# First attention of a hybrid block: the side work of TensorE in pieces behind even chunks, v in another bank, routing spread over three batches, and the bias table loaded in the tail

## What is computed

```python
scores = g_scale * jnp.einsum('bhqd,bhkd->bhqk', l2norm(q), l2norm(k))         # attn_a
pos = jnp.cumsum(ohf, axis=0) - 1.0; keep = posk < C                           # routing
scores = jnp.einsum('bqhd,bkhd->bhqk', q, k) * scale + position_bias           # attn_b
```

## Time and profile before

| | us |
|---|---|
| median of 3 runs | 1488.24 |
| lowest and highest run | 1486.22, 1497.35 |
| the profiled execution: its own time | 1500.14 |
| its span, first to last instruction | 1498.4 |
| PE busy | 1257.2 (84%) |
| DVE busy | 933.7 (62%) |
| ACT busy | 871.3 (58%) |
| POOL busy | 511.1 (34%) |

### The profile page before, as it was taken

The page is one execution under the profiler, slowest core; times in us unless marked ns, Lnnn a source line. Parts: engine busy times, 40 slices in busy tenths (PEclk is TensorE's granted clock), DMA queues, the critical chain, the costliest instruction groups (busy, mean ns, idle before and its releaser), DMA issues.

```text
span 1498.4 us, 22434 instructions
## 1 busy us (share of the span) xinstructions
PE 1257.2 (84%) x6711; PEld 634.5 (42%) x6711; DVE 933.7 (62%) x2823; ACT 871.3 (58%) x1716; POOL 511.1 (34%) x788
## 2 busy tenths in 40 slices
PE   3888888888749399999999999998999999997292
PEld 2333323332237144454554544544544544544172
DVE  5344555554311278779788698798788788784210
ACT  1777777777514176766656566676566567562041
POOL 2001222222426323323432443343443434424244
PEclk7898999998859699999999999999999999999597
DMA  5554432226349246656656666576575665568322
GB/s 159 113 171 162 131 123 82 89 95 199 97 98 169 51 106 154 161 137 155 166 122 144 166 150 149 132 166 149 136 166 122 149 156 144 117 145 222 83 24 23
DMA packets 132936, 197.91 MB, mean 132 GB/s; under 512 B 35166, under 2 KB 76077, under 8 KB 132816
## 3 DMA queue, kind: packets, MB, share of 16 engines
q1 hardware_dynamic: 104848, 138.67, 35.8%
q0 software_dynamic: 27392, 56.76, 17.9%
q10 hardware_dynamic: 576, 1.05, 0.2%
HBM read 61.75 MB, written 39.24 MB: 67 GB/s over the span
## 4 chain that ended last, share of the span: by engine, by line
PE 64%; DVE 11%; issue 7%; DMA 6%; ACT 6%; POOL 3%; SPq 1%; DVEq 0%; POOLq 0%; ACTq 0%
PE s_ps L1387 13%; PE o_psb L1407 7%; PE o_ps L879 6%; PE o_psb L1412 6%; ACT probs_a L619 5%; PE score_ps L865 4%; PE m_ps L1361 4%; PE m_ps L1378 4%; PE r_ps L1421 3%; PE r_ps L1378 3%; DVE tile L1610 3%; PE p_ps L1395 3%; DVE blocks L1623 2%; DMA x_mid<-o_g_f,rows_f 2%; PE t_ps L894 1%
## 5 line engine op out<-in xcount | busy, mean ns | idle before, releaser
L1523 ACT ACTIVATE tile<-tile,low 128x512 f32<-128x512 f32 x512 | 363.8, 714 | 263.9 <-DVE low L1610 255.0
L1304 POOL DMA_DIRECT2D crossed<-blocks x512 | 253.7, 506 | 505.2 <-DVE blocks L1623 463.5
L1610 DVE CUSTOM_DVE_ANT_0 tile<-s_ps,bias 128x512 f32<-128x512 f32 x512 | 330.5, 682 | 48.7 <-PE s_ps L1387 38.1
L619 ACT ACTIVATE probs_a<-score_ps,gbound 128x1024 f32<-128x1024 f32 x256 | 268.7, 1113 | 105.8 <-PE score_ps L865 105.4
L1387 PE MATMUL s_ps<-kT,qT 64*128 64x512 f32 x1024 | 269.4, 634 | 24.3 <-DVE low L1610 16.6
L1623 DVE STREAM_TRANSPOSE blocks<-tile 128x512 f32<-128x512 f32 x384 | 256.6, 694 | 0.0
L1407 PE MATMUL o_psb<-crossed,v_b 128*64 128x512 f32 x512 | 236.6, 605 | 9.1 <-DMA crossed<-blocks 7.9
L338 POOL DMA_INDIRECT slots<-rows_r,slot_r x128 | 127.8, 998 | 86.7 <-issue 55.0
L879 PE MATMUL o_ps<-probs_a,v_ext 128*32 128x512 f32 x1024 | 153.2, 674 | 0.5 <-ACT probs_a L619 0.5
L1387 PEld LDWEIGHTS s_ps<-kT,qT 64*128 64x128 f32 x1024 | 86.3, 188 | 141.0 <-issue 87.0
L865 PE MATMUL score_ps<-q_stack,k_stack 32*128 32x512 f32 x512 | 100.3, 545 | 39.6 <-ACT probs_a L619 23.4
(11 more groups left out here) (160 smaller groups left out, 1622.4 us busy)
## 6 DMA issues: line engine op xcount, KB each, us to landing
crossed<-blocks SPq DMA_DIRECT2D x512, 96.0 KB
crossed<-blocks POOLq DMA_DIRECT2D x512, 96.0 KB
inv_row<-inv_rows SPq DMA_DIRECT2D x128, 128.0 KB
q_parts<-parts SPq DMA_DIRECT2D x32, 256.0 KB, 3.9
k_stack<-k_parts SPq DMA_DIRECT2D x32, 256.0 KB, 4.4
q_stack<-q_parts SPq DMA_DIRECT2D x32, 256.0 KB, 4.8
w_f<-in_w SPq DMA_DIRECT2D x32, 256.0 KB, 6.4
k_parts<-parts SPq DMA_DIRECT2D x28, 256.0 KB, 4.0
```

What stands on the lines that cost most here:

```text
L619: nc.scalar.activation(probs[q % 2][:, c % 4 // 2, pair:pair + 2, :].rearrange("p h t -> p (h t)"), score_ps[c % 2][:, :], ACT.Exp, bias=g ...
L1304: pool.dma_start(strip_to(n, a, m), strip_from(n, a, m)).then_inc(crossed_sw[n % 2], 16)
L1523: nc.scalar.activation(tile[(b * NS + k) % RING][s][:, :], tile[(b * NS + k) % RING][s][:, :], ACT.Exp, bias=low[n % 2][:, s, i:i + 1], sc ...
L1610: nc.vector.tensor_tensor_reduce(out=tile[(b * NS + k) % RING][s][:, :], in0=s_ps[k % 2][s][:, :], in1=bias[:, h, off:off + S], scale=1.0, ...
```

## The change

- **PE's order in the first attention.** The constants move all side work behind even chunks, between the scores of the two chunks of a pair: x turned behind chunk 0, q and k in two halves behind 2 and 4, v behind 6, q and k turned behind 16; `to_tokens` behind 10 (group 3 of the batch before), 18, 22 and 30; the router's counts behind 22, turn behind 26, logits behind 28. Each `to_tokens` now stands some chunks after the copy that it needs.
- **Banks.** v is made in `t_ps` instead of the upper half of `aux_ps`; so q and k no longer wait for v's copy, and group 3's `to_tokens` waits for it instead. `take` gains a wait for the turn of the group before.
- **Routing over three batches.** Turn, logits and exps stay one batch behind (b - 1); picks, counts and addresses are done two batches behind (b - 2), in the middle of DVE's list. A second signal, `late`, carries those steps. The scatter of batch b - 2 stands behind groups 2 and 3 (three pieces each), its last two pieces in the next batch. In the last batch all that is left is done in a denser order.
- **DVE's list** is rewritten accordingly; the normed rows of batch b + 2 are made at the end of batch b; the Newton steps are split around `take(b, 0)`. SQUARE_AT goes from 9 to 5.
- **Bias table.** Its place in the memory is that of the first attention's q and k buffers. SP loads 6 of its 8 parts when the last scores are done, ahead of the store of the last batch's x, and the last 2 behind the experts' rows.
- **Second attention.** DVE picks the first expert at the end of step 26 and the second at the end of step 28 (both were at 27); ACT's router exp stands at the start of step 26 instead of its end.

```diff
@@ -120,8 +120,8 @@
 
     STATS, MOMENTS, VAR, ROWS, TURNED = TB, 2 * TB, 2 * TB + 1, 3 * TB + 1, 3 * TB + 2
     TOP, SHIFTED = TURNED + 1, TURNED + 2
-    FIRST, SECOND = SHIFTED + 1, SHIFTED + 7
-    CHOSEN = SHIFTED + 12
+    FIRST, SECOND = 1, 7
...
@@ -152,7 +152,8 @@
         self.m, self.addr = own("m", [P, TOPK, TB]), own("addr", [P, TOPK, TB])
         self.slot = [own(f"slot{n}", [P, TOPK, TB], I32) for n in range(bufs)]
         self.const, self.w_in = sem(f"r_const{f}"), sem(f"r_w_in{f}")
-        self.step = Signal(sem(f"r_step{f}"), self.SLOTS)
+        self.step = Signal(sem(f"r_step{f}"), self.SHIFTED)
+        self.late = Signal(sem(f"r_late{f}"), self.SLOTS)
...
@@ -416,9 +421,11 @@
         stacks_in = [Signal(sem(f"stacks_in{i}"), 16 * 2) for i in range(GROUPS)]
         NCH = 32
 
-        AT_PE, SQUARE_AT = [3, 5, 7, 17], 9
-        ROUTE_MORE = dict(turn=23, logits=25, exps=28, counts=31)
-        ROUTE_LAST = dict(turn=13, logits=15, exps=18, counts=25)
+        SQUARE_AT = 5
+        TURN_X, QK_FIRST, QK_SECOND, MAKE_V, TURN_QK = 0, 2, 4, 6, 16
+        TOKENS_MORE, TOKENS_LAST = {10: -1, 18: 0, 22: 1, 30: 2}, {6: -1, 14: 0, 22: 1, 30: 2}
+        ROUTE_MORE = dict(counts=22, turn=26, logits=28, exps=30)
+        ROUTE_LAST = dict(counts=8, turn=18, logits=20, exps=22, own_counts=28)
...
@@ -547,20 +554,21 @@
                 nc.gpsimd.tensor_tensor(rstd[:, lo:hi], var[:, lo:hi], g["neg_half"][:, 0:hi - lo],
                                         ALU.pow).then_inc(ln_rstd, 1)
 
-            def batch(b, before):
-                if before:
-                    r.inverse_std(pool, b - 1)
+            def batch(b):
                 wait(pool, v_staged, b + 1, 1)
                 for grp in range(GROUPS):
                     wait(pool, av_done, b, 2 * grp + 2)
                     pool.sem_inc(g["passed_pool"], 1)
                     move_v(grp)
-                    if b >= 2:
-                        r.scatter(pool, b - 2, range(2 * grp, 2 * grp + 2))
-                    if before and grp == 0:
+                    if grp == 0 and b >= 3:
+                        r.scatter(pool, b - 3, range(6, 8))
+                    if grp == 1 and b >= 3:
+                        r.landed(pool, b - 3)
+                    if grp == 1 and b >= 1:
+                        r.inverse_std(pool, b - 1)
                         r.copy_rows(pool, b - 1)
-                if b >= 2:
-                    r.landed(pool, b - 2)
+                    if grp >= 2 and b >= 2:
...
@@ -718,6 +735,10 @@
 
             def take(b, grp):
                 wait(dve, av_done, b, 2 * grp + 2)
+                if grp >= 1:
+                    wait(dve, oT_ps, b, grp)
+                elif b >= 1:
+                    wait(dve, oT_ps, b - 1, GROUPS)
...
@@ -736,42 +757,57 @@
             turned, logits = aux_ps[:, 0:S], aux_ps[:, S:S + TB * E_N].rearrange("p (t e) -> p t e", e=E_N)
             counts = aux_ps[:, S + TB * E_N:S + 2 * TB * E_N].rearrange("p (t e) -> p t e", e=E_N)
 
-            def batch(b, before):
-                prepare(b + 1, 0)
-                if before:
+            def batch(b):
+                prepare(b + 1, 1)
+                if b >= 2:
+                    r.pick(dve, b - 2, 0)
+                    r.pick(dve, b - 2, 1)
+                if b >= 1:
                     take(b - 1, 3)
-                prepare(b + 1, 1)
-                if before:
+                if b >= 2:
+                    r.run_counts(dve, b - 2)
+                    r.weigh(dve, b - 2)
+                prepare(b + 1, 3)
+                prepare(b + 1, 2)
+                prepare(b + 1, 4)
+                take(b, 0)
+                prepare(b + 1, 5)
+                if b >= 1:
                     finish(b - 1, 3)
                     wait(dve, res_done, b - 1, GROUPS)
                     r.norm_stats(dve, b - 1)
-                prepare(b + 1, 2)
-                if before:
+                prepare(b + 1, 6)
+                take(b, 1)
+                if b >= 1:
                     r.norm_moments(dve, b - 1)
-                take(b, 0)
-                prepare(b + 1, 3)
                 finish(b, 0)
-                if before:
+                if b >= 2:
+                    r.take_counts(dve, b - 2, counts)
+                    r.address(dve, b - 2)
+                if b >= 1:
                     r.norm_rows(dve, b - 1)
-                take(b, 1)
-                prepare(b + 1, 4)
                 finish(b, 1)
-                if before:
+                if b >= 1:
                     r.copy_turned(dve, b - 1, turned)
                 take(b, 2)
-                if before:
+                if b >= 1:
                     r.shift(dve, b - 1, logits)
+                if b + 2 < B:
+                    prepare(b + 2, 0)
                 finish(b, 2)
-                if before:
-                    r.select(dve, b - 1)
-                    r.locate(dve, b - 1, counts)
 
...
@@ -818,38 +856,43 @@
...
+            def turn_x(b):
+                wait(pe, xn_ready, b, TB)
+                wait(pe, rest_ready, 0, b)
+                if b >= 3:
...
+                    last = nc.tensor.transpose(aux_ps[:, i * P:(i + 1) * P], xn[:, i, :], g["ident"][:, :])
+                last.then_inc(xT_ps.sem, 1)
+
+            def make_qk(b, tiles):
+                wait(pe, xT_ready, b, 1)
+                if b >= 3:
+                    wait(pe, r.step, b - 3, r.SHIFTED)
+                for i in tiles:
+                    last = nc.tensor.matmul(aux_ps[:, i * 2 * D:(i + 1) * 2 * D], xT[:, i * P:(i + 1) * P],
...
+            def make_v(b):
+                wait(pe, xT_ready, b, 1)
+                if b >= 1:
+                    wait(pe, v_staged, b - 1, 1)
+                if b >= 2:
+                    wait(pe, on_step, b - 2, 2 * (GROUPS - 1))
...
-                        wait(pe, v_staged, b, 1)
-                    for i in range(TB):
...
             def to_tokens(b, grp):
                 wait(pe, o_copied, b, grp + 1)
+                if grp == GROUPS - 1:
+                    wait(pe, v_staged, 0, min(b + 3, B))
...
+                    to_tokens(b, grp)
+                elif b >= 1:
+                    to_tokens(b - 1, GROUPS - 1)
+
             def attend(b, before, more):
                 at = ROUTE_MORE if more else ROUTE_LAST
...
-                        to_tokens(b - 1, GROUPS - 1)
-                    if q >= 3 and q % 2 == 1:
-                        to_tokens(b, (q - 3) // 2)
                     for part in range(4):
...
@@ -913,13 +974,17 @@
                                 values(b, q - 1, part // 2)
                             elif before:
                                 values(b - 1, 7, part // 2)
-                        if more and c in AT_PE:
-                            prepare(b + 1, AT_PE.index(c))
+                        if more:
+                            extras(b, c)
+                        if c in tokens_at:
+                            tokens(b, tokens_at[c])
+                        if b >= 2 and c == at["counts"]:
+                            r.counts(pe, b - 2, counts, lambda: wait(pe, rest_ready, 0, min(b + 2, B)))
                         if before and c == at["turn"]:
-                            r.turn(pe, b - 1, turned, lambda: wait(pe, rest_ready, 0, b + 2) if more else None)
+                            r.turn(pe, b - 1, turned, lambda: wait(pe, rest_ready, 0, min(b + 2, B)))
                         if before and c == at["logits"]:
                             r.logits(pe, b - 1, logits, lambda: None)
-                        if before and c == at["counts"]:
...
@@ -944,19 +1010,34 @@
             r.logits(pe, B - 1, logits, lambda: None)
...
+        def load_bias(sp, parts):
+            for n in parts:
+                low = P - 1 - n
+                part = flat[:, low:low + COPIES * (REL - step)].rearrange("h (p r) -> p h r", r=REL - step)[:, :, 0:WREL]
+                sp.dma_start(bias[n:P:step, :, :], part).then_inc(g["wb"]["loaded"], 16)
+
         def before_rows(sp):
             wb = g["wb"]
             for name in ("wv", "wq", "wk"):
                 sp.dma_start(wb[name][:, :], g["b_W" + name[1]]).then_inc(wb["loaded"], 16)
             sp.dma_start(wb["wo"][:, :, :], g["b_Wo"].rearrange("(n p) d -> p n d", p=P)).then_inc(wb["loaded"], 16)
+            sp.wait_ge(cleared, 16 * (1 + 2 * B))
+            wait(sp, s_ready, B - 1, NCH)
+            sp.sem_inc(g["passed_sp"], 1)
+            load_bias(sp, range(0, step - 2))
             store_rows(sp, B - 1)
-            sp.wait_ge(cleared, 16 * (1 + 2 * B))
             sp.wait_ge(x_stored, 16 * B)
             sp.wait_ge(e_in, 32)
             wait(sp, r.scattered, B - 1, r.scattered.per)
             sp.sem_inc(g["passed_sp"], 1)
 
-        return before_rows
+        def rest(sp):
+            load_bias(sp, range(step - 2, step))
+
+        return dict(rows=before_rows, rest=rest)
 
...
@@ -1003,14 +1084,7 @@
```

(21 more changed lines are left out.)

205 lines of the change are left out of this document (109 added, 96 removed).

## The result

The changed kernel takes 1423.18 us (median of 4 runs, 1422.84 to 1426.35) against 1492.16 for the kernel before on the same chip (1486.22 to 1497.35). The ratio is 0.954, 95% interval 0.951 to 0.957: 4.6% faster. Run again later (experiment 9) it gave 1425.16 against 1493.38, ratio 0.952 (0.949 to 0.956). The prediction was 1438, range 1422 to 1462, so the measured time lies inside it by 1 us. The profiled execution of the changed kernel took 1422.84 with a span of 1421.1, 77.3 less than the span of before.

A forecast was written before the change was run, and what follows sets the result against it. In the first attention neither PE nor ACT was full; both waited on the hand-over of scores, with low clock second. Gains of 42 + 0 + 5 + 6 = 53, 50 kept against the median: 1488.2 - 50 = 1438 us, range 1422 to 1462.

The forecast's parts named there:

- The five free pairs: Middle batches, first attention: five of 16 pairs without a piece, 2.05 us each, or 1.44 if PE catches up fully.
- the price of an odd chunk: First attention: side work behind an odd chunk delays the next scores by its full length; behind an even one PE uses its wait.
- I kept back 5 us: First attention: 2 us of the last batch's gain and 3 of the six middle batches' given back for low clock.
- The first rival: First attention: the clock keeps falling in a loop that PE fills, leaving 29 to 32 of 53 us, 1458; chance 0.18.
- The 3 kept back against the median: Whole kernel: only 50 of the 53 us counted against the median, as the profiled execution stood 12 us above it.
- Parts without a charge: First attention: DVE's new order and POOL's scatters cost nothing; SP's later queue has 5 us of cover.
- the stacks: First attention rival: split q and k arrive late and bound the batch, 8 us, giving 1446; chance 0.07.
- my step: First attention, middle batches: PE's pieces counted pair by pair give 39.8 us a batch, 35 us gained over six.
- First and last batch: First attention: the first batch gains 3 us, the last 9.4.
- the charge of 4 for the low clock: First batch: 4 us charged because the low clock of the start now meets the four densest pairs.
- Tail and experts: Tail: 0, bias parts and store end some 4 us early at 214 GB/s; experts: 5 us from POOL's removed wait.
- Second attention: Moving the first pick lets DVE reach step 29 about 1.0 us earlier in six places: 6 us, ends 8 and 0.

The follow-up runs named there:

- experiment 9: The changed kernel run again without an edit: 1425.16 us against 1493.38 for the kernel before, ratio 0.952.
- experiment 4: The changed kernel with each piece of PE's side work one chunk later, behind odd chunks: ratio 0.960 to the kernel before, batches of 41.2 us.
- experiments 7 and 11: The changed kernel with v ahead of q and k in their bank; in the second, DVE also copies v ahead of the picks: ratios 0.977 and 0.973.
- experiment 8: The changed kernel with the first batch's side work two chunks later and one POOL wait removed from the tail: ratio 0.958 to the kernel before.
- experiment 1: The changed kernel with the second attention's routing put back where it was: ratio 0.963 to the kernel before.
- experiment 10: The changed kernel with PE waiting for the same chunk's exp at chunks 27 to 31 in batches 1 to 6: ratio 0.987 to the kernel before.
- experiment 7: The changed kernel with v projected ahead of q and k into their bank, DVE copying v ahead of the reduction: ratio 0.977 to the kernel before.
- experiment 5: The changed kernel with PE waiting for the same chunk's exp at chunks 11, 19, 25 and 31 in batches 1 to 6: ratio 0.966.

## Why the prediction was right, and where its sizes were not

*The bound.* Right: PE's side work behind even chunks fills its gaps. ACT's idle time in middle batches comes in pieces of at most 0.4, and a middle batch is 39.0 where I had 39.8 between 37.1 and 40.2. The five free pairs, priced at 1.44 to 2.05, took 1.72 to 2.14 each in the batch from 193.7 on: PE catches up in them by part only. Two of the `to_tokens` stand three chunks behind the values that they follow, not four as I wrote; no middle batch waits there. My account of the price of an odd chunk was incomplete: of the 4.7 us that PE idles a batch in experiment 4, 2.1 are the copy of `o_sb`.

*The low clock.* Here the sizing failed. I kept back 5 us of the gain against low-clock stretches in mid-batch. Nothing was to be given back: from 76.9 us to the end of the loop all is at full clock, in the profiled execution and in that of the repetition. The 273.8 us of the middle batches had 0.92 of it. At full clock they would have been some 6 x 44.4 = 266, so by this estimate about 7 of the 40 us are the clock's, and I had given the clock no term on the side of the gain. The first rival (chance 0.18) had weighed the right sign: "those at a batch's start came right behind the counts' wait". With that wait and those for `o_sb` gone the falls went. As experiment 8 has one without a wait, some of this may be luck. The 3 kept back against the median had the right sign and were too few: 77.3 us lie between the profiled executions, 69.0 between the medians. The kernel before varies with its clock: in the later runs its executions took 1489 to 1491 us with a mean clock of 0.932 and 1501 to 1506 with 0.919.

*Parts without a charge.* DVE's new order, POOL's scatters and SP's queue cost next to nothing (PE waits 0.2 a batch for one copy of `o_sb`), and the stacks were never late. But the working gave the bank of v no term at all, and it was worth some 30 us that my step counted under the pieces: without it PE waits for a copy in every batch, 2.6 us or so, and the low clock comes back (experiments 7 and 11). That the total came out near is in part luck.

*First and last batch.* 4.5 and 9.9 against 3 and 9.4. The sum for the first batch has a slip: 44.1 - 38 - 4 leaves 2, not 3. The batch took 39.7, 1.7 above the 38 at full clock, so the charge of 4 for the low clock was too high; the same first batch took 39.3 to 42.3 in the other runs that leave it alone. PE's wait for the normed rows wasn't what holds it: without that wait (experiment 8) it was no shorter.

*Tail and experts.* -0.9 against 0 and 6.0 against 5. The 0.9 is POOL's wait for the landing of the second last batch's rows, which the transfers of the table delay: removed, it gave 0.85. The load ran at about 195 GB/s, not 214, so it and the store ended at 376 instead of 4 us before they were needed: my margin was gone, and two parts more showed what lies behind it.

*Second attention.* The step that was most off: 6 against 17.7. DVE in the same batch as the earlier trace rows:

```profile
629.57 0.18 DVE L226 TENSOR_REDUCE m_r<-ex_r 128x4 f32<-128x32 f32 x1
...
630.90 0.69 DVE L1710 TENSOR_TENSOR ctxT<-o_psb,inv_row 128x512 f32<-128x512 f32 x1
...
635.78 0.65 DVE L1683 CUSTOM_DVE_ANT_0 tile<-s_ps,bias 128x512 f32<-128x512 f32 x1
...
640.44 0.14 DVE L226 TENSOR_REDUCE m_r<-ex_r 128x4 f32<-128x32 f32 x1
```

In the earlier trace rows it is 8.00 us from `ctxT` (689.50) to the first lowest of step 28 (697.50), here 4.88. The four steps ahead of step 28 take 23.8 us in each routed batch and took 26.3 or more: 2.5 are won. The second pick gives 1.1 back ahead of step 29. That leaves 1.4 a batch, not 1.0, and seven routed batches, not six: 10 us. The remaining 7 or 8 I had not priced; in the traces there stand the waits for the copied x, 9 us less in sum, and with them the clock's falls. I had read these waits as one delay that the pick's 1.0 would shorten. Three of the six long ones (four in experiment 1) were followed by a stretch at half speed. How the 7 or 8 divide between the waits and the clock isn't shown.

## What to carry to other kernels

Price waits of a busy TensorE at more than their length when they stand close together: here the clock fell behind waits of 1.2 us in company each time, and that cost as much again as the waits, up to three times as much (batches of 45 to 50 us instead of 39.0, with 3.4 us of idle time in the one of 50.4). It isn't a rule for a single wait: most of 1.0 left the clock alone, and some of 0.8 did not. Side work belongs between the two operations whose results the next engine takes in turn, where it also covers a copy; and a buffer move whose only effect is that a wait lies on no one's way can be worth more than the instructions moved. A transfer put ahead of a deadline is free up to the deadline and costs its full length from there on: count bytes by the rate seen there, with the store queued behind it.

## What the runs showed of the hardware

- TensorE's clock went from 2.4 to 1.2 GHz in loops in which PE was busy for 83% and more. It did so at or right behind waits of 0.81 (before, three places), 1.07 (before, five of six places), 1.21 behind 0.51 (experiment 10, six of six), 1.95 (second attention, before and in experiment 1, seven of the twelve waits of 1.8 and more) and 2.73 us (experiment 7, four places), and once with no wait in the eight us before (experiment 8). In the middle batches it stayed up with four spread gaps of up to 0.93 in a batch (experiment 5, one trace), and in five batches with PE idle for 4.7 us of 41.2 in pieces of up to 1.04 (experiment 4). The length of the last wait alone doesn't sort these cases. The Trainium skill ("TensorE: Matmul & The Clock Gate", section "HAM oscillation — how this bites in real kernels") puts such falls down to idle gaps far longer; this case's traces do not agree. Its next section, "A second HAM failure mode: psum-queue depth-cycling", has the clock oscillate by short idle stretches between groups of matmuls when they are frequent. The bunched gaps of experiment 10 agree with that; experiments 4 and 5, with short gaps all through the batch and one fall in their middle batches together, show that being frequent isn't enough.
- A matmul group of eight at 1.2 GHz takes 1.94 us against 1.06, 1.8 times as long.
- In the tail the queues moved 190 to 210 GB/s for most of the time, with the table's parts and the store as nearly all of their bytes (6.00 of 6.01 MB from 345 to 381 us), no more than with the experts' rows and scatter-adds beside them (214 in the earlier trace rows).
